# V's projection with proxy and gate columns, and record rows by one-hot products on TensorE, in a convolution, attention and mixture-of-experts kernel

## What is computed

```python
# 1: self-attention over the pixels of an image, with q and k of 32 channels
q, k, v = Wq @ xf + bq, Wk @ xf + bk, Wv @ xf + bv
x = alpha * (v @ softmax(q.T @ k).T) + x
# 2: attention by 16 proxies, cumulative over the tokens
n = layernorm(t)
prods = proxy @ n                                   # (b, 16, s)
y = cumsum(prods[..., None] * n[:, None], axis=2)
t = t + einsum('bps,bpsd->bsd', softmax(prods / 4, axis=1), y)
# 3: eight experts, two for each token
f = layernorm(t)
top_vals, top_idx = top_k(f @ gate_w.T, 2)
combine = one_hot(top_idx) weighted by softmax(top_vals)
t = t + sum_e combine[:, e] * (gelu(f @ w1[e] + b1[e]) @ w2[e] + b2[e])
```

## Time and profile before

| | |
|---|---|
| median of 3 runs | 883.59 us |
| lowest, highest | 874.88, 887.90 us |
| profiled execution | 888.49 us, span 886.7 us |
| stage A | 0 to 220 us |
| stage B | 220 to 427 us |
| stage C | 427 to 886.7 us |
| PE busy / share of the span | 791.0 us / 89% |
| DVE | 468.3 us / 53% |
| POOL | 420.8 us / 47% |
| ACT | 324.8 us / 37% |

### The profile page before, as it was taken

The page is one execution under the profiler, slowest core; times in us unless marked ns, Lnnn a source line. Parts: engine busy times, 40 slices in busy tenths (PEclk is TensorE's granted clock), DMA queues, the critical chain, the costliest instruction groups (busy, mean ns, idle before and its releaser), DMA issues.

```text
span 886.7 us, 18873 instructions
## 1 busy us (share of the span) xinstructions
PE 791.0 (89%) x5745; PEld 720.2 (81%) x5746; DVE 468.3 (53%) x982; ACT 324.8 (37%) x588; POOL 420.8 (47%) x405
## 2 busy tenths in 40 slices
PE   4998989897899999961299999999999999999993
PEld 3887978787567666631299999999999999999993
DVE  3777878877335365643045454454545444454541
ACT  2764747375233334220132333323233332223330
POOL 2474745456112366447324555445555544555332
PEclk9999999999655597865599999999999999999998
DMA  8576594856311111220117565265755626555222
GB/s 292 181 291 285 180 418 159 331 213 225 135 48 48 48 48 48 72 65 8 54 32 238 144 190 180 43 228 142 234 144 182 184 42 231 142 142 142 25 25 27
DMA packets 47724, 130.03 MB, mean 147 GB/s; under 512 B 7104, under 2 KB 37184, under 8 KB 43072
## 3 DMA queue, kind: packets, MB, share of 16 engines
q1 hardware_dynamic: 30288, 104.74, 31.7%
q0 software_dynamic: 16032, 19.49, 12.8%
q10 hardware_dynamic: 1360, 5.24, 1.6%
HBM read 186.52 MB, written 47.79 MB: 264 GB/s over the span
## 4 chain that ended last, share of the span: by engine, by line
PE 48%; DMA 1%; issue 1%; POOL 1%; DVE 0%; POOLq 0%; ACT 0%; DVEq 0%
PE ps_h L68 8%; PE ps_h L69 8%; PE ps_h L70 8%; PE ps_y L70 8%; PE ps_y L69 8%; PE ps_y L68 8%; PE ps_x L1331 2%; DMA out_tok<-y,to_row 0%; POOL out_tok L1218 0%; DMA records<-places 0%; DMA x_rows<-normed,from_row 0%; POOLq L1139 0%; DVE yb L1292 0%; DVE xtl L1278 0%; ACT xth L1244 0%
## 5 line engine op out<-in xcount | busy, mean ns | idle before, releaser
L1253 ACT ACTIVATE g<-ps_h,bias 128x256 f32<-128x256 f32 x288 | 120.7, 471 | 282.6 <-PE ps_h L70 282.6
L1218 POOL DMA_INDIRECT out_tok<-y,to_row x72 | 124.5, 1730 | 155.7 <-DVE y L1299 134.3
L68 PE MATMUL ps_h<-xth,wbuf 128*128 128x256 f32 x576 | 164.7, 286 | 3.3 <-issue 1.8
L68 PE MATMUL ps_y<-wbuf,gl 128*128 x576 | 165.6, 288 | 0.0
L69 PE MATMUL ps_h<-xtl,wbuf 128*128 128x256 f32 x576 | 164.4, 285 | 0.0
L70 PE MATMUL ps_h<-xth,wbuf 128*128 128x256 f32 x576 | 164.3, 285 | 0.0
L70 PE MATMUL ps_y<-wbuf,gh 128*128 x576 | 163.2, 283 | 0.0
L69 PE MATMUL ps_y<-wbuf,gh 128*128 x576 | 163.0, 283 | 0.0
L68 PEld LDWEIGHTS ps_h<-xth,wbuf 128*128 128x128 f32 x576 | 112.0, 195 | 3.9 <-issue 2.1
L69 PEld LDWEIGHTS ps_h<-xtl,wbuf 128*128 128x128 f32 x576 | 112.1, 195 | 0.0
L70 PEld LDWEIGHTS ps_h<-xth,wbuf 128*128 128x128 f32 x576 | 112.0, 194 | 0.0
(11 more groups left out here) (189 smaller groups left out, 1403.3 us busy)
## 6 DMA issues: line engine op xcount, KB each, us to landing
wbuf<-wsplit SPq DMA_DIRECT2D x71, 2048.0 KB, 8.8
wsplit<-wbuf SPq DMA_DIRECT2D x14, 2048.0 KB, 12.0
wraw<-in_w SPq DMA_DIRECT2D x16, 1024.0 KB, 7.5
xraw<-in_x_ch ACTq DMA_DIRECT2D x5, 1024.0 KB, 11.0
tok<-in_x_tok SPq DMA_DIRECT2D x1, 4096.0 KB, 17.0
out_tok<-tok SPq DMA_DIRECT2D x8, 512.0 KB
normed<-x SPq DMA_DIRECT2D x8, 512.0 KB, 2.9
x_rows<-normed,from_row POOLq DMA_INDIRECT x72, 3.2
```

What stands on the lines that cost most here:

```text
L68: eng.matmul(out, ll, rh, start=first, stop=False)
L1218: pool.indirect_dma_start(out=out, out_offset=bass.IndirectOffsetOnAxis(ap=to_row[:, par, s:s + 1], axis=0), in_=y[:, par, s, :], in_offse ...
L1253: last = act.activation(g[:, f, :], ps_h[:, q, f % 2, :], ACT.Gelu_apprx_tanh, bias=bias1[:, bass.ds(e, 1), f:f + 1].rearrange("p a f -> p ...
```

## The change

Stage A projects on the proxies and the gate along with V. Since layer 1's output is a weighted sum of V plus x, its product with the 24 proxy and gate columns is the same weighted sum of V's products plus x's. So `wv` is extended by `wv.T @ [proxy, gate]` (24 columns, made on the chip in `extend`) and by `[proxy, gate]` itself (24 more, for the residual). V tiles and `tok` become 280 wide (`CW`), V's projection 304 (`VW`). The layer norm enters afterwards by each token's mean and deviation (`Tokens.products` on POOL), and the softmax over proxies is done in three batches (`softmax_in`, `exponential`, `softmax_out`).

Stage B loses the turnings of rows, both projections, and the second norm's turning; the gate columns ride along as 8 more columns of the state and output products (264, `XW`). `norm1` and `norm2` as classes go. The state lives on 128 partitions with one weight matrix of 128 columns per image. Instead of DRAM scatters, `record` adds up one-hot products in PSUM: for each of the eight (choice, image) pairs a lane mask times a cell mask, 16 products of 256 columns a chunk, and `decode` turns the sums into `records` in SBUF. The share goes into eight extra columns of `normed`, and stage C takes it from the gathered row (`keep_share`). Stage C otherwise stays.

```diff
@@ stage_a
-        no_token, zero_row = sb("no_token", [P, COLS, 2], I32), sb("zero_row", [P, PAD // P, C])
+            sp.dma_start(wv_nat, wv.rearrange("(k p) m -> p k m", p=P)).then_inc(ext_in, 16)
+            sp.dma_start(wv_raw[:, :, CW:CW + NP], proxy_t.rearrange("(k p) n -> p k n", p=P)).then_inc(ext_in, 16)
+            sp.dma_start(wv_raw[:, :, CW + NP:VW], gate_t.rearrange("(k p) n -> p k n", p=P)).then_inc(ext_in, 16)
+            sp.dma_start(bv_col, bv_t).then_inc(ext_in, 16)
...
+                    pool.tensor_copy(mine[:, js, :], vf[:, ch % 2, :, CW:VW])
+                    pool.tensor_tensor(vl[:, js, :], vf[:, ch % 2, :, 0:CW], vh[:, js, :].bitcast(F32),
+                                       ALU.subtract).then_inc(v_ok, 1)
...
-                        if not more and (par, part) == (1, 0):
-                            pool.wait_ge(norm_set, 3)
-                            norm1.scale_and_shift(pool, 0)
+                        if not more and par == 0:
+                            tok.products(pool, fixed, *BATCHES[part], part)
...
+                if it:
+                    statistics(g - 1)
...
+            extend()
...
-                    if ch == 2:
+                    if ch == 1:
                         pe.wait_ge(added, done(b * IT - 1))
+                    if ch >= 2:
+                        pe.wait_ge(v_full, done(b * 4 + ch - 2))
...
-                        last = mm3(pe, ps_o[it % 2][:, 0:C], (pth[:, it % 2, j], ptl[:, it % 2, j]),
+                        last = mm3(pe, ps_o[:, it % 2, 0:CW], (pth[:, it % 2, j], ptl[:, it % 2, j]),
@@ stage_b, POOL
+            def combine(c, par):
+
+                pool.wait_ge(w1_d, done(c))
+                pool.tensor_tensor(share[:, 1, :], gap_exp[:, :], share[:, 0, :], ALU.mult).then_inc(w2_d, 1)
...
+            def mark_lanes(c, par):
+
+                wait_apart(pool, spot_d, done(c))
+                wait_apart(pool, rec_mm, done(c - 2))
+                lanes = lane_id[:, :]
+                for k in range(2):
+                    for b in range(B):
+                        mine = spot[:, 0, k * B + b:k * B + b + 1]
+                        pool.tensor_scalar(lane_tile[:, par, k * B + b, :], lanes, mine, tile_no[:, b:b + 1],
+                                           ALU.is_equal, ALU.mult)
+                        last = pool.tensor_scalar(lane_part[:, par, k * B + b, :], lanes, mine, part_id[:, 0:1],
+                                                  ALU.is_equal, ALU.mult)
+                last.then_inc(lane_d, 1)
...
             def body(i, par):
...
+                if exists(i - 1):
+                    relative_gap(i - 1)
+                if exists(i + 2):
+                    prepare(i + 2, par)
+                if exists(i - 1):
+                    combine(i - 1, 1 - par)
+                    count(i - 1, 1 - par)
+                    mark_lanes(i - 1, 1 - par)
+                if exists(i):
+                    normalise(i)
@@ stage_b, DVE
+            def mark_cells(c, par):
+
+                dve.wait_ge(spot_d, done(c))
+                dve.wait_ge(rec_mm, done(c - 2))
+                for kb in range(KB):
+                    last = dve.tensor_scalar(cell[:, par, kb, :], column_id[:, :], spot[:, 1, kb:kb + 1], None, ALU.is_equal)
+                last.then_inc(cell_d, 1)
...
             def body(i, par):
...
+                if exists(i):
+                    add_out(i)
+                if exists(i - 1):
+                    read_rank(i - 1)
+                if exists(i):
+                    statistics(i)
+                if exists(i - 1):
+                    rank_chosen(i - 1, 1 - par)
+                if exists(i + 1):
+                    mask(i + 1)
...
@@ stage_b, PE
+            def record(c, par):
+
+                pe.wait_ge(lane_d, done(c))
+                pe.wait_ge(cell_d, done(c))
+                for kb in range(KB):
+                    end = isinstance(c, int) and c == CH - 1 and kb == KB - 1
+                    pe.matmul(ps_rec[:, 0:CELLS], lane_tile[:, par, kb, :], cell[:, par, kb, :], start=False, stop=False)
+                    last = pe.matmul(ps_rec[:, CELLS:2 * CELLS], lane_part[:, par, kb, :], cell[:, par, kb, :],
+                                     start=False, stop=end)
+                last.then_inc(rec_mm, 1)
...
+                if exists(i):
+                    output(i, par)
+                if exists(i - 1):
+                    rank_choices(i - 1, 1 - par)
+                if exists(i - 2):
+                    record(i - 2, par)
+                if exists(i + 1):
+                    attend(i + 1, 1 - par)
+                if exists(i + 2):
+                    turn(i + 2)
@@ stage_c
-            sp.dma_start(records[:, :, :].rearrange("p g r -> p (g r)"),
-                         places.rearrange("(p g) r -> p (g r)", p=P)).then_inc(records_in, 16)
...
+            def keep_share(u, slot):
+
+                e = entry(dve, T_EXPERT, u, E - 1)
+                dve.wait_ge(x_in[slot], (before(u, slot) + 1) * 32)
+                dve.tensor_copy(share[:, slot, :], x[:, slot, :, bass.ds(C + e, 1)].rearrange("p s a -> p (s a)")).then_inc(share_d, 1)
```

More of the change, by code:

```diff
@@ L86, in __init__ @@
[L86 to L127, removed]
@@ L492, in image @@
                         stack(b + 1, 0)
-                    if not more and it == 3:
-                        dve.wait_ge(added, done(b * IT))
-                        norm1.statistics(dve, chunk_tiles(tok, 0), 0)
+                    if it == IT - 1:
+                        statistics(g)
+                    if not more:
+                        routing_weights(it)
             stack(0, 0)
@@ L650, in stage_b @@
-        biases_in, counted, table_step, second_in = sems("biases_in counted table_step second_in")
-        prod_d, pmax_d, prel_d, psum_d, prec_d, pw_d = sems(
-            "prod prod_max prod_rel prod_sum prod_recip prod_w")
-        attn_d, tok_d, state_d, logit_d, top_d, topid_d = sems(
-            "attn tok state logit top top_id")
-        topf_d, hot_d, chose_d, newly_d, count_d, rank_d, hotrank_d, placef_d, place_d = sems(
-            "top_f hot chose newly count rank hot_rank place_f place")
@@ L738, in _ @@
+            pool.iota(records[:, CELLS:COLS], pattern=[[0, (COLS - CELLS) // 2], [P, 2]], base=TOK, channel_multiplier=1
+                      ).then_inc(routing_set, 1)
+            pool.wait_ge(routing_set, 2)
+            tok.products(pool, fixed, *BATCHES[2], 2)
+            for i in range(-1, 2):
+                body(i, i % 2)
+            middle_and_end(pool, body)
         @block.scalar
         def _(act):
-            for s in (norm2.done, xt1_d, pexp_d, pw_turned_d, xt2_d, gexp_d):
+            for s in (turned_d, x1_d, gexp_d, x2_d):
@@ L753, in body, with apply @@
[L753 to L761 removed]
+            def apply(dst, tiles, inv_std, shift):
+                for b in range(B):
+                    last = act.activation(dst[:, b, 0:C], tiles[:, b, :], ACT.Identity, bias=shift[:, b:b + 1],
+                                          scale=inv_std[:, b:b + 1])
+                return last
@@ L772, in body @@
[L772 to L780 removed]
+                if exists(i + 2):
+                    first_norm(i + 2, par)
@@ L892, in body @@
-            def body(i, par):
-                near, far, new = i + 1, i + 2, i + 3
-                if exists(near):
-                    mask(near)
-                if exists(new):
-                    norm1.statistics(dve, chunk_tiles(tok, new), new)
-                if exists(i - 1):
-                    find_places(i - 1, 1 - par)
-                if exists(near):
-                    grow_state(near, 1 - par)
-                if exists(far):
-                    proxy_softmax_in(far, par)
-                    proxy_softmax_out(far)
-                if exists(near):
-                    add_out(near)
-                    dve.wait_ge(tok_d, done(near))
-                    norm2.statistics(dve, chunk_tiles(tok, near), near)
+                dve.tensor_tensor(chose[:, par], hot[:, par, 0], hot[:, par, 1], ALU.add).then_inc(chose_d, 1)
@@ L1059, in _ @@
+            for i in range(-2, 2):
+                if i == 1:
+                    pe.wait_ge(routing_set, 2)
+                body(i, i % 2)
+            middle_and_end(pe, body)
             pe.wait_ge(count_d, done(CH - 1))
-            pe.wait_ge(logit_d, done(CH - 1))
-            pe.matmul(ps_count, fixed.ones[:, :], counts_m[:, :], start=True, stop=True).then_inc(counted, 1)
+            pe.wait_ge(attn_d, done(CH - 1))
+            pe.matmul(ps_count, ones[:, :], counts_m[:, :], start=True, stop=True).then_inc(counted, 1)
```

836 lines of the change are left out of this document (491 added, 345 removed).

## The result

| | before | changed |
|---|---|---|
| median | 880.9 us (4 runs of the same session) | 897.28 us (4 runs, 895.41 to 897.95) |
| ratio | | 1.018, 95% interval 1.010 to 1.026 |
| profiled execution, span | 886.7 us | 895.6 us |
| stage A ends | 220.0 | 242.5 |
| first output added, after B's start | 26 | 18.1 |

855 was forecast, in a range of 836 to 885. The time lies above the range and on the other side of no change. The interval leaves no change outside, but it is open whether the kernel is slower by over 2%.

What follows compares the result with a forecast made beforehand. Stage A was taken as bound by a full TensorE, stage B's chunks as a fixed PE sequence at half or full clock. 888.5 + 16 - 33.5 - 11 = 860, less 4.9 to the median: 855 us, range 836 to 885.

Steps and rivals of the forecast that it cites:

- B's start to the first output: Stage B: first output at 26 us as before, no projection ahead but constants' setup and the last products batch on POOL.
- chunks 1 and 2: Stage B's first chunks: at half clock without full record work, 17 us each.
- 16 one-hot operations of 128 elements in `mark_lanes`, 0.28 each by the nearest row: POOL in stage B: masks cost 4.5 us a chunk, within a POOL total of 8.5.
- The rival: POOL's one-hot operations cost p, not 0.28; p = 0.9 eats the whole gain, 1.1 gives 904 us; chance 0.08.
- twice 0.28: Stage B on POOL: the prediction is wrong if mark_lanes operations take twice the forecast 0.28 us.
- 14.5: Stage B: forecast pitch in us of each of five later chunks at full clock, range 11.5 to 16.
- All three come to about 11.5 at full clock, so waits now decide. I add 3: Stage B chunk: PE, DVE and POOL sequences about 11.5 us, plus 3 for DVE operations held up by mark_lanes.
- `count` and `mark_lanes(7)` to 21: Tail: POOL's combine, count and last mask set end 21 us after the last output, within a 41 us tail.
- Full clock from chunk 3 on: Stage B: denser record and attend bring clock 1.00 from chunk 3, with tok stores 13 to 16 us apart.
- Rival 1: Stage B: the clock stays down, PE bounds chunks at 20.5 us, total 885, no change; chance 0.20.
- the +4: Stage A: if weight loads set the spacing, added columns grow A by about 4 us and not 12.
- The top is POOL: `products` for 24 tiles is queued ahead of `w_lo`: Stage A's end: SP's last stores and closing wait come later; part of a +2 term (1 to 9).

Runs made afterwards that it cites:

- The three orders: Changed kernel's own order, 897.28 us; with normalise ahead of mark_lanes on POOL, 906.1; with also attend and turn ahead of record on PE, 887.5.
- the spare work: Changed kernel with all masks on DVE, plus eighteen POOL operations a chunk that nobody reads: 877.8 us in a single execution.
- the fastest kernel: Changed kernel with twelve masks on DVE, four on POOL, both products batches behind w_lo, and attend and turn ahead of record on PE: 822.4 us.

## Why the prediction was wrong

Its own sum, against the profiled execution (860 forecast there, 895.6 + 1.8 = 897.4 measured):

| term | forecast | measured | difference |
|---|---|---|---|
| stage A | +16 | +22.5 | +6.5 |
| B's start to the first output | 26 | 18.1 | -7.9 |
| chunks 1 and 2 | 34 | 16.2 | -17.8 |
| five chunks | 72.5 | 106.1 | +33.6 |
| tail | 41 | 67.3 | +26.3 |
| stage C | 0 | -3.3 | -3.3 |
| | 860 | 897.4 | +37.4 |

Three terms came out lower than forecast, by 29.0 together, 25.7 of it ahead of chunk 3. That was luck: without it the miss would be 66. The other three, +66.4, are the price of a mask (9.5 in the chunks and 7.9 in the tail), the waits that the ring adds in the chunks (24), the sets of masks that were not counted in the tail (with what stands behind them, 18) and stage A (6.5).

**The price of a mask.** The step "16 one-hot operations of 128 elements in `mark_lanes`, 0.28 each by the nearest row" failed: they start 0.774 apart. The row was of another operation, with no per-partition scalar and one step. The rival named the right unknown and asked of it only whether it passes 0.9. Its sign of being wrong, twice 0.28, came true.

**A sum where a ring was.** This is the larger error. With the measured price the prediction's own formula gives POOL's cycle as 4 + 16 x 0.774 = 16.4 (POOL's work was 16.7), a pitch 1.9 above 14.5 and a tail 7.9 longer: 860 + 9.5 + 7.9 = 877.4, and 872.5 after the 4.9 to the median, still 1% faster than before and within the range. The step that failed is "All three come to about 11.5 at full clock, so waits now decide. I add 3": it took the largest of three engines' sums and priced the waits as contention. The masks wait for the spots of DVE, and DVE's next statistics wait for `normalise`, which stands behind the masks in POOL's queue. So 12.8 adds to a ring of 21.2 and does not lie beside DVE's 10.4 to 12.0. The three orders and the spare work show it. Both facts were in the change: the order of POOL's `body`, and the wait of `statistics`.

**The tail.** "`count` and `mark_lanes(7)` to 21" counted one set of masks. At the last output (382.91) the set of chunk 5 is just under way, it ends at 393.4, and those of chunks 6 and 7 are still to come: together 35.6 of the 67.3 us. With most or all masks on DVE the tail is 37.8 to 38.3 in six kernels, against 41 forecast, so the other terms of that step were about right.

**What held, and the clock.** With the masks on DVE the pitch was 14.2, against 14.5. That the two agree is in part luck, since 14.5 was for a DVE without them. Full clock from chunk 3 on did not come: it was 1.00 from 261 to 277 in the changed kernel, but then a mean of 0.74, no higher than the 0.78 of the same five chunks before (296.8 to 386). It was 0.86 with all masks on DVE and 0.94 in the fastest kernel, where PE idles less than in the changed one. Rival 1 did not decide the time either: PE was busy 52 of the 106 us. An output product at full clock is 0.445 for its two passes, from 336.40 to 339.96 for eight, where 0.64 was put.

**Chunks 1 and 2, and the setup.** Half clock was forecast for these chunks, 17 each. They took 7.3 and 8.9 at full clock, with no set of masks in front of them. The 26 us to the first output set the lost projections off against new setup work and POOL's `products`; by the trace the 26 were 7.9 too many.

**Stage A.** Columns were right: neighbours of 280 columns are 0.13 apart, and of V's 304 columns 0.14, some 0.4 to 0.5 ns a column above; the start was +1.2 (12.41 against 11.20 for the first q/k product). The Trainium skill (TensorE: Matmul & The Clock Gate, LDWEIGHTS) states only how long a weight load takes. That the added columns would hide behind it was the prediction's reading; the trace shows them paid, and the +4 was wrong. What went wrong is "The top is POOL: `products` for 24 tiles is queued ahead of `w_lo`": the place was right, the price of 1 to 9 was meant for the last store, while the damage came through the weight load and ACT, 10.3 us of PE. Inside `products` one operation, the power of 24 elements, took 4.20 us.

**Left open.** Stage C is 3.3 us shorter in the changed kernel, and no run was made on it. Whether 12.05 can be lowered by other splits was not tried. Nor was the other way out of the ring: DVE's statistics wait for `shift2` because `stat2` and `mv2` exist once, and a second copy of them might let that wait go.

## What to carry to other kernels

Before summing up an engine's work, follow the ring of one iteration through the in-order queues: a block adds its full length to the ring when a small operation that the block's own producer needs stands behind it, though no engine is full. Moving it within the queue changed which small operation was late and gained 10 us at best; shortening it, or splitting it off to the engine that makes its input, paid 61 us. Price a new form of instruction by a row of the same operation on the same engine, and where none exists, let the range hold two or three times the nearest row in every place where it is issued, the tail included.

## What was not expected of the hardware

- On POOL, `tensor_scalar` over 128 x 128 with two per-partition scalars takes 0.78 us in bf16 and in float32 alike, 0.60 with one comparison; on DVE the bf16 form starts every 0.22. The Trainium skill (GPSIMD Engine Reference, Engine selection) puts POOL at about line rate for one input; here it is 3.5 times DVE.
- A power on POOL takes 4.20 us for 24 elements a partition and 1.02 for 4: 0.16 an element.
- The kernel before has no fixed time: its stage B, PE-bound, took 151 or 166 us to the last output in two profiles, at a mean granted clock of 0.75 and 0.68. The changed kernel, where PE is half busy there, repeats within 0.3%.
